# Moving event picks, event rows and event factors forward in VectorE's program, and ScalarE's sines ahead of its search

## What is computed

```python
def _build_mat(rots, idx_i, idx_j, ndim):
    def step(mat, t):
        i, j, theta = t
        c = jnp.cos(theta)
        s = jnp.sin(theta)
        ri = mat[i]
        rj = mat[j]
        mat = mat.at[i].set(c * ri - s * rj)
        mat = mat.at[j].set(s * ri + c * rj)
        return (mat, None)
    mat0 = jnp.eye(ndim, dtype=rots.dtype)
    mat, _ = jax.lax.scan(step, mat0, (idx_i, idx_j, rots))
    return mat.T
...
xn = _layernorm(x, axis=-1)
x = x + _L0_gnn_ref(xn, edge_weight, src, dst) + _L0_mix_ref(xn[None], ...)[0]
x = x + _L0_ffn_ref(_layernorm(x, axis=-1)[None], ...)[0]
```

## Time and profile before

| | |
|---|---|
| three runs, median (lowest to highest) | 763.93 us (762.85 to 764.43) |
| the profiled execution | 764.22 us, its span 762.4 us |
| TensorE busy | 649.5 us (85%) |
| VectorE busy | 508.6 us (67%) |
| ScalarE busy | 443.9 us (58%) |
| GpSimd busy | 407.6 us (53%) |
| chain that ended last | TensorE 60%, VectorE 21%, no visible cause 7%, transfers 4%, ScalarE 3% |

### The profile page before, as it was taken

One profiled execution on the slowest core, in us unless ns is written; L12 is line 12 of the kernel. 1 busy time (PEld: TensorE's weight loads), 2 busy tenths in 40 slices (PEclk: granted clock), 3 DMA queues, 4 the chain that ended last, 5 costly groups with the idle time before them and its releaser, 6 DMA issues.

```text
span 762.4 us, 18086 instructions
## 1 busy us (share of the span) xinstructions
PE 649.5 (85%) x4055; PEld 552.4 (72%) x4056; DVE 508.6 (67%) x1934; ACT 443.9 (58%) x1218; POOL 407.6 (53%) x494
## 2 busy tenths in 40 slices
PE   6679799944369898807999999999979999999997
PEld 5356467632257666506998999899969999999996
DVE  4999758869957688853454444444446777777775
ACT  6446676557313177844666666566645666666663
POOL 7763777235411237770666677523335666666655
PEclk7879899975579999957999999999999999999999
DMA  6802011415620045562344333322213333333322
GB/s 197 257 2 85 19 33 27 122 52 190 202 71 1 29 144 183 192 209 65 120 141 135 115 131 118 103 69 69 67 63 101 99 104 102 98 103 101 110 91 65
DMA packets 60749, 79.72 MB, mean 105 GB/s; under 512 B 15719, under 2 KB 49381, under 8 KB 60319
## 3 DMA queue, kind: packets, MB, share of 16 engines
q1 hardware_dynamic: 45145, 43.27, 19.6%
q0 software_dynamic: 14976, 35.38, 13.9%
q10 hardware_dynamic: 576, 0.54, 0.2%
HBM read 47.53 MB, written 33.13 MB: 106 GB/s over the span
## 4 chain that ended last, share of the span: by engine, by line
PE 60%; DVE 21%; issue 7%; DMA 4%; ACT 3%; POOL 2%; SPq 1%; DVEq 1%; POOLq 0%; ACTq 0%
PE banks L2601 22%; PE banks L2611 20%; PE banks L2229 4%; PE banks L2208 3%; PE banks L2592 3%; PE banks L2553 2%; DVE R L1997 2%; DVE R L1742 1%; DVE R L1420 1%; DMA R<-in_x_dram 1%; DVE topi L2023 1%; DVE R L1757 1%; DVE R L1302 1%; DMA R<-send_d 1%; PE banks L2219 1%
## 5 line engine op out<-in xcount | busy, mean ns | idle before, releaser
L2601 PE MATMUL banks<-R 128*128 128x128 f32 x1696 | 210.1, 278 | 2.8 <-ACT R L1251 2.8
L2601 PEld LDWEIGHTS banks<-R 128*128 128x128 f32 x1696 | 200.7, 194 | 3.7 <-ACT R L1251 3.6
L2611 PE MATMUL banks<-R 128*128 x848 | 200.7, 380 | 0.0
L1264 ACT ACTIVATE R<-banks,b1c 128x128 f32<-128x128 f32 x424 | 143.5, 365 | 52.0 <-PE banks L2601 51.8
L2611 PEld LDWEIGHTS banks<-R 128*128 128x128 f32 x848 | 153.4, 191 | 16.5
L1251 ACT ACTIVATE R<-banks,bet_c,gam_c 128x128 f32<-128x128 f32 x212 | 85.7, 454 | 106.1 <-PE banks L2592 103.3
L2116 DVE COPY R<-R 128x1024 f32 x106 | 74.5, 702 | 77.2 <-PE banks L2601 60.9
L899 POOL DMA_INDIRECT send_d<-R,slot_all x98 | 97.1, 991 | 48.1 <-issue 40.8
L912 POOL DMA_INDIRECT first_d<-R,dest_now x54 | 60.7, 1123 | 93.3 <-DVE R L2121 81.7
L921 POOL DMA_INDIRECT R<-first_d,get_now x52 | 53.8, 1034 | 50.6 <-DVE get_now L2098 46.3
L912 POOL DMA_INDIRECT out_dram<-R,dest_now x52 | 64.4, 1239 | 30.4 <-issue 27.1
(11 more groups left out here) (545 smaller groups left out, 998.4 us busy)
## 6 DMA issues: line engine op xcount, KB each, us to landing
R<-send_d SPq DMA_DIRECT2D x106, 131.0 KB
R<-in_L_ffn_W_dram SPq DMA_DIRECT2D x16, 512.0 KB, 4.5
R<-in_x_dram SPq DMA_DIRECT2D x14, 512.0 KB, 4.3
R<-in_x_dram SPq DMA_DIRECT2D x5, 1024.0 KB, 10.8
send_d<-zrow SPq DMA_DIRECT2D x14, 131.0 KB, 2.4
send_d<-R,slot_all POOLq DMA_INDIRECT x98, 3.1
erec_d<-R SPq DMA_DIRECT2D x1, 1400.0 KB
rec_d<-R SPq DMA_DIRECT2D x1, 1400.0 KB
```

The costliest lines, as they stand in the source:

```text
L1264: last = nc.scalar.activation(hT[b][:, c, :], bank[2 + 2 * b + c // 2][:, (c % 2) * P:(c % 2 + 1) * P], ACT.Gelu, bias=b1c[:, bass.ds(e, 1 ...
L2601: last = mm(bank[2 + 2 * b + c // 2][:, (c % 2) * P:(c % 2 + 1) * P], w1c[b][:, kb, c * P:(c + 1) * P], xmT[b][:, kb * P:(kb + 1) * P], st ...
L2611: last = mm(bank[6 + b][:, 0:D], hT[b][:, c, :], w2s[:, bass.ds(e, 1), c, :].rearrange("p a h -> p (a h)"), start=(c == 0), stop=(c == H / ...
```

## The change

1. On VectorE, `pick_head` moves from behind mixing step 10 to ahead of it. `event_rows` moves from behind step 11 to ahead of it. The two copies that start `Mrot` and the wait for the last normalised rows move from behind step 10 to behind step 11.
2. The constants of the chunk stage and `event_factors` move ahead of `weighted_sum(12)`, which waits for the last weighted product. So that the constants may be written while that product still reads `xng`, `matched`, which is used later, changes places with `placed` in R4.
3. On ScalarE, the sines move ahead of `search`.
4. The unused `t_at`, one small instruction of `event_rows`, goes.

```diff
@@ buffers
-        w_lo, w_hi, t_of, t_at, not_t, rank, is_pair, second, valid, ahead_by, span, same, both_in, factor_of, cos_of, sin_of, sign_of, less_of = [found_at(NCH) for _ in range(18)]
+        w_lo, w_hi, t_of, not_t, rank, is_pair, second, valid, ahead_by, span, same, both_in, factor_of, cos_of, sin_of, sign_of, less_of = [found_at(NCH) for _ in range(17)]
...
         onehot = tabled(RING, D, dt=BF16)
+        matched = tabled(2, CK * (CK + 1) // 2 * P, dt=BF16)
+        assert tabled.at >= 4 * D
         placed = tabled(RING_P, 2 + WIDE * HK, dt=BF16)
-        matched = tabled(2, CK * (CK + 1) // 2 * P, dt=BF16)
@@ ScalarE
             turned_exps(NG12)
-            search()
             act.wait_ge(S["edge_dve"], PICKED)
...
+            search()
             search_in()
@@ VectorE
-                TS(t_at, t_of, -1.0, None, ALU.add)
...
+            pick_head()
             mix_step(NG12 - 2)
+            event_rows()
+            mix_step(NG12 - 1)
             for kb in range(KB):
                 last = nc.vector.tensor_copy(Mrot[:, kb, kb * P:(kb + 1) * P], ident[:, :])
             last.then_inc(S["M_ready"], 1)
             dve.wait_ge(S["xn_ready"], NG12 + 1)
-            pick_head()
-            mix_step(NG12 - 1)
-            event_rows()
             mix_step(NG12)
-            weighted_sum(NG12)
             nc.vector.tensor_copy(rows16, t_of)
...
             event_factors()
+            weighted_sum(NG12)
             rank_rows(0)
```

## The result

| | before | after |
|---|---|---|
| median (lowest to highest), 13 runs each | 762.73 us (757.41 to 764.43) | 766.22 us (761.87 to 769.20) |
| ratio, with its 95% interval | | 1.0065 (1.0041 to 1.0090) |
| the profiled execution, its span | 764.22, 762.4 us | 765.33, 763.5 us |

The changed kernel is slower by 0.65% (the medians of the table differ by 3.5 us, the means by 4.2). As differences of means the three are 4.2, 2.5 and 3.4 us, +3.4 together, where +0.9 was forecast. The 766.22 us lie inside the forecast's 762.8 to 767.2, but only since the three runs that it started from stood at 763.93, 1.2 us above the median of all thirteen.

The account below looks back on a forecast made before the run. The prediction took the bound to be when VectorE leaves the chunk loop, after a chain of waits with TensorE and ScalarE. Terms 2.9 - 0.8 - 3.2 + 2.0 gave +0.9 us on the median 763.93: 764.8 us, range 762.8 to 767.2.

Parts of the forecast that it names:

- the 0.2% that the forecast called most likely: Whole kernel: no measurable change, within about 0.2% (1.5 us) of the kernel before; chance 0.66.
- Part 1: Head's picks ahead of mixing step 10: TensorE's turns of group 11 come 2.9 us later.
- the arithmetic of the ring: Mixing steps on VectorE, ScalarE, TensorE: picks of 3.37 us delay the turns 2.9 us, idling TensorE 2.3 us.
- no wait of their own: Picks ahead of step 10: gathers land at 138.4, just before 138.6; a late landing costs up to 1 us.
- The clock, priced as a rival: TensorE's clock falls in the new idle before step 10's product: turns 2.7 us more, total +3.6, 767.5; chance 0.10.
- Part 2: Event rows ahead of mixing step 11: they no longer delay product 12, so 0.8 us comes back.
- Part 3: Constants and factors in the wait for product 12: TensorE's 3.2 us of idle behind that product goes.
- Part 4: ScalarE's search behind the sines: later one-hot rows hold back chunk 6 and take back 2.0 us.
- The sum: Whole kernel: 2.9 - 0.8 - 3.2 + 2.0 = +0.9 us.

Follow-up runs that it names:

- filled_short: Changed kernel with ten unused matrix products on TensorE in the new idle time before the product of step 10; ratio 1.0038 to the kernel before.
- search_first: Changed kernel with ScalarE's search put back ahead of the sines; ratio 1.0044 to the kernel before.
- picks_alone: Kernel before with only `pick_head` moved ahead of mixing step 10; 767.61 us against 761.92, ratio 1.0067; its repeat was a single execution.
- swap_alone: Kernel before with only ScalarE's sines moved ahead of its search; ratio 1.0003.
- early_search: Changed kernel with picks and event rows back in their old places and search ahead of group 12's exponentials; ratio 0.9976 to the kernel before, repeated 0.9972.
- late_picks: Changed kernel with picks and event rows back in their old places; 759.98 us, ratio 0.9973 to the kernel before, repeated 0.9953.
- after_again: The changed kernel measured a second time, same code; 764.38 us, ratio 1.0023 to the kernel before.

## Why the prediction was wrong

The forecast was +0.9 us, within 0.2% of the kernel before; measured are +0.65% and, in two repetitions, +0.23% and +0.30%. The sign was right, the size off by 2.5 us, and +0.65% lies outside the 0.2% that the forecast called most likely.

- **Part 1, the arithmetic of the ring: right.** +2.9 us to the turns of group 11 forecast, +3.1 where neither clock nor gathers interfered (`filled_short`). TensorE's idle was 2.49 (2.3 forecast).
- **Part 1, "no wait of their own": wrong.** It rested on a margin of 0.2 us between a landing reckoned for 138.4 and a start at 138.6, both read from one trace in which the third pick was slow (2.76). In four of the eight traces with early picks it was fast, the last gather was issued 1.3 to 1.5 us later as well, and the picks waited 2.6 to 2.9 us for the landing, of which 0.8 reach the turns (8.2 against 7.5). The text gave it "up to 1 us", which is the size, but took it for the exception.
- **The clock, priced as a rival with a chance of 0.10: this is the step that failed.** I took the 1.90 us of idle in the earlier trace rows, behind which the product kept its speed, as nearest to the new 2.3 us, and left the clock out of the sum. It fell in five of six traces. Its price was given as 2.7 us of delay for a product of 6.72 us; measured are 1.3 us of turns in the short pattern (8.7 and 8.8 against 7.5) and 2.8 in the long one (10.9 to 11.1 against 8.2 in `search_first`). So the price was twice that of the short pattern and right for the long one, and the chance was off by a factor of eight. The trace of before had two nearer falls that I passed over. One is the spread at 162.10 in the earlier trace rows itself, behind 3.17 us of idle. The other is an earlier product, ahead of which the granted clock was 1.00 and in whose first 2 us it was 0.53:

```profile
55.35 5.38 PE L2229 MATMUL banks<-R 128*128 128x256 f32 x16 [3.18 <-DVE R L1360]
```

The new 2.3 us lie between the 1.90 that held and the 3.17 that fell, and those rows give no ground for 0.10. The 5.38 us of the row above are also just what the short pattern has.

- **Part 2, -0.8: right.** Product 12 waits 1.18 us for ScalarE in after and 1.92 for VectorE in `picks_alone`, where the event rows stayed: 0.74 us.
- **Part 3, -3.2: right.** The idle time behind product 12 is gone in all kernels that have it together with part 4.
- **Part 4, +2.0: right in its mechanism.** First one-hot row 171.06 - 158.31 = 12.75 us behind product 12, forecast 12.7. By itself it binds nothing (`swap_alone`), and with the search out of the way chunk 6 comes 2.1 us sooner (`early_search`). The table load took 1.28 us and the sine followed at once, as in the earlier trace rows. The Trainium skill ("ScalarE: Activation LUTs", section "What ACT_TABLE_LOAD costs") budgets 2.66 us for it; no run here shows the drain.
- **The sum.** With the turns of the three traces of the changed kernel at 10.2 us as a mean, part 1 costs 5.9 us instead of 2.9, and the sum is +3.9; chunk 6 stands +4.1 later as a mean (36.9 against 32.7), the first combined product +4.4 (124.3, 127.0 and 126.9 us behind the anchor, against 121.6), and the times say +3.4. From that product to the end the fourteen traces took 498.9 to 502.0 us (501.0 before; 500.1, 498.9 and 501.6 in the changed kernel), in no order that follows the edits. The 1 us between trace and time is well inside that spread, whose cause stays open.

That the profiled execution came out at 765.33 us, where its own forecast was 765.1, is chance: it had the short pattern, and its execution reached the anchor 0.6 us sooner.

Open stays what decides whether the clock falls in a given execution. `search_first` kept it through 3.39 us of idle, `early_search_2` lost it after two gaps of 1.59 and 1.18 us, and ahead of product 12 1.92 us lost it in `picks_alone` and not in `picks_alone_2` or `swap_alone`. The length alone doesn't decide: ahead of the earlier product quoted above a gap of 2.49 us held in `early_search`, as long as the one that fell ahead of step 10 in after.

## What to carry to other kernels

Work that is put ahead of an instruction for which TensorE waits can cost twice: its own length, and what TensorE loses at the lower clock behind the gap. Before a new gap of 2 us or more is accepted, list every gap of the trace with the duration of what followed it, and not the nearest one alone. Here one fell behind 3.2 us and one held behind 1.9; a new gap between them can't be priced as one that holds. Put the fall into the sum, or fill or avoid the gap. A margin of a few tenths of a microsecond between a landing and its reader, read from one execution, is a coin's toss: here it held in four of eight traces. And of a change in several parts, time each with the others undone: here one part lost up to 0.7% and hid a gain of 0.3 to 0.5% in the rest.

## What the runs showed of the hardware

- Ahead of the product of step 10 a gap of 2.5 us on TensorE was followed by 5.38 us for a product of 3.62 (two traces of two), one of 3.5 us by 6.59, 6.68 and 6.61, once by 3.69. Ahead of an earlier product (the one at 55.35 us in before) gaps of 2.00 to 2.49 us were followed by 3.69 us in seven traces, and gaps of 2.97 to 3.60 us by 5.16 to 6.71 us in the other seven. The same gap has no fixed price: it differs between places and between executions. One of those that held, in `late_picks_2`:

```profile
50.81 3.69 PE L2228 MATMUL banks<-R 128*128 128x256 f32 x16 [2.48 <-DVE R L1360]
```

- VectorE's pick over 128x704 and GpSimd's product over 125x800 slow each other: 2.75 and 2.76 us where they overlap, 1.48 and 1.90 us where they don't. In after the pick started first (134.17), and at its usual length would have ended just ahead of the product (135.86), beside GpSimd's L855; which of the two drew it out isn't shown. The last gather's issue took 1.40 us where the pick had started 0.85 us before it (`after_again`), and 0.94 where the issue started first (after).
- Executions of one kernel differ by up to 4.3 us already at the anchor (138.50 and 134.21 in two traces of `late_picks`), which hides most of what one change of this size does. That is why stages are compared here, and not spans.
